# Expert biases read from SBUF at a register's address, in place of two transfers per tile

## What is computed

```python
def _moe(tokens, router_w, w1, b1, w2, b2):
    logits = tokens @ router_w.T
    probs = jax.nn.softmax(logits, axis=-1)
    rw, re = jax.lax.top_k(probs, TOP_K)            # TOP_K = 2, 8 experts
    ...
    for e in range(E):
        h = jax.nn.gelu(tokens @ w1[e] + b1[e], approximate=False)
        y = h @ w2[e] + b2[e]
        out = out + combine[:, e:e + 1] * y
    return out
```

## Time and profile before

| | us |
|---|---|
| median of three runs | 1556.3 (1552.33 to 1566.34) |
| span of the profiled execution | 1438.5 |
| median less span | 117.8 |
| TensorE busy in the span | 1290.5 (90%) |
| VectorE busy | 1128.0 (78%) |
| ScalarE busy | 991.0 (69%) |
| GpSimd busy | 753.0 (52%) |

### The profile page before, as it was taken

The page is one execution under the profiler, slowest core; times in us unless marked ns, Lnnn a source line. Parts: engine busy times, 40 slices in busy tenths (PEclk is TensorE's granted clock), DMA queues, the critical chain, the costliest instruction groups (busy, mean ns, idle before and its releaser), DMA issues. The chain is left out here.

```text
span 1438.5 us, 28829 instructions
## 1 busy us (share of the span) xinstructions
PE 1290.5 (90%) x8512; PEld 1130.8 (79%) x8512; DVE 1128.0 (78%) x3903; ACT 991.0 (69%) x2090; POOL 753.0 (52%) x963
## 2 busy tenths in 40 slices
PE   3899999999999999999999489999999999994544
PEld 3788888888888888888887378899999999993433
DVE  5478888888788878778786888899999999993332
ACT  1777677767677777676765567788888888871332
POOL 3115655666555575656555575566666666663000
PEclk9999999999999999999999779999999999996555
DMA  8622534353542222222111189988888888865999
GB/s 279 212 81 79 146 89 135 101 150 85 139 130 68 79 79 67 80 72 77 56 53 43 49 263 318 289 277 269 271 279 264 272 279 269 268 220 225 425 424 378
DMA packets 144136, 264.00 MB, mean 184 GB/s; under 512 B 52336, under 2 KB 74480, under 8 KB 139760
## 3 DMA queue, kind: packets, MB, share of 16 engines
q1 hardware_dynamic: 113440, 173.78, 38.6%
q0 software_dynamic: 25920, 71.60, 14.0%
q10 hardware_dynamic: 4624, 16.78, 2.9%
HBM read 128.39 MB, written 100.68 MB: 159 GB/s over the span
## 5 line engine op out<-in xcount | busy, mean ns | idle before, releaser
L1716 POOL DMA_INDIRECT answers<-yy,dest_i x284 | 280.3, 987 | 175.2 <-DVE yy L1837 100.8
L1558 POOL DMA_INDIRECT sent<-tn,slot_s x256 | 276.4, 1080 | 146.1 <-issue 79.3
L1768 PE MATMUL s_bank<-band,hh 128*128 x568 | 163.2, 287 | 0.6 <-DVE yy L1872 0.6
L1768 PE MATMUL s_bank<-w_s,hh 128*128 x568 | 157.2, 277 | 0.0
L1768 PE MATMUL s_bank<-band,hl 128*128 x568 | 157.0, 276 | 0.0
L1802 ACT ACTIVATE hid<-m_bank,b1s 128x512 f32<-128x512 f32 x142 | 97.9, 689 | 80.7 <-PE m_bank L1751 48.3
L1822 ACT ACTIVATE zz<-xin 128x256 f32<-128x256 f32 x284 | 147.5, 601 | 0.0
L758 PE MATMUL m_bank<-wvo,band 128*128 128x258 f32 x792 | 132.7, 303 | 13.2 <-DVE band L1390 10.9
L1535 POOL TENSOR_TENSOR rs<-ve,halves 128x4 f32<-128x4 f32 x64 | 65.0, 1020 | 150.8 <-DVE ve L1252 150.8
L790 PE MATMUL o_bank<-vv,at 128*128 128x256 f32 x512 | 140.8, 398 | 1.4 <-DVE tt L1300 0.7
L758 PEld LDWEIGHTS m_bank<-wvo,band 128*128 128x128 f32 x792 | 107.0, 191 | 29.5 <-issue 27.8
(11 more groups left out here) (238 smaller groups left out, 3655.9 us busy)
## 6 DMA issues: line engine op xcount, KB each, us to landing
xin<-sent SPq DMA_DIRECT2D x71, 524.0 KB
got<-answers SPq DMA_DIRECT2D x32, 1024.0 KB, 13.8
w1hs<-rT SPq DMA_DIRECT2D x71, 256.0 KB
w1ls<-w_s SPq DMA_DIRECT2D x71, 256.0 KB
xs<-in_x SPq DMA_DIRECT2D x32, 512.0 KB, 4.8
raw<-in_x SPq DMA_DIRECT2D x32, 512.0 KB
out_x<-fin ACTq DMA_DIRECT2D x15, 1024.0 KB, 12.4
b2s<-in_b SPq DMA_DIRECT2D x71, 128.0 KB
```

Source lines behind the costliest of these rows:

```text
L1558: eng.indirect_dma_start(sent, bass.IndirectOffsetOnAxis(slot_s[:, par, j, k:k + 1], 0), tn[:, par, k, :], None).then_inc(scattered[par], 16)
L1716: eng.indirect_dma_start(answers, bass.IndirectOffsetOnAxis(dest_i[:, at_ % RING, k:k + 1], 0), yy[:, slot, k, :], None).then_inc(rows_out ...
L1768: last = eng.matmul(y_bank[half][:, k * C:(k + 1) * C], hx[:, par, f, ts], rhs, start=(n == 0), stop=(n == 3 * CC - 1))
```

## The change

`b1_all`, the table of all experts' b1, has been in SBUF since the token loop. ScalarE now takes its bias from there: it loads the tile's expert into a register of its own and reads at that address. `b2_all` is a new buffer of 8 KB per partition in place of `b2s` (4 KB); SyncE fills it once, behind tile 0's weights, with one transfer of 1 MB that copies the whole of b2 to all partitions. VectorE also loads the expert's number itself and reads `b2_all` at that address. SyncE's transfers of `b1s` and `b2s` are gone; `w_here` counts 32 per tile in place of 64. The waits of ScalarE and VectorE on `w_here` are gone; VectorE waits for `b2_in` once.

```diff
-        b1s = eb("b1s", [P, WS, CC])
-        b2s = eb("b2s", [P, WS, C])
+        b2_all = eb("b2_all", [P, E, C])
+        b2_in = sem("b2_in")
...
-                    eng.dma_start(b1s[:, slot, :], b1_all[:, bass.ds(e, 1), :].rearrange("p e a -> p (e a)"))\
-                       .then_inc(w_here[slot], 16)
-                    eng.dma_start(b2s[:, slot, :], b2[bass.ds(e, 1), :].rearrange("e c -> (e c)").partition_broadcast(P))\
-                       .then_inc(w_here[slot], 16)
+                    if at_ == 0:
+                        eng.dma_start(b2_all[:, :, :].rearrange(flat), b2.rearrange("e c -> (e c)").partition_broadcast(P))\
+                           .then_inc(b2_in, 16)
...
-                    eng.wait_ge(w_here[at_ % WS], at_ // WS * 64 + 64)
+                    eng.wait_ge(w_here[at_ % WS], at_ // WS * 32 + 32)
...
-                    eng.wait_ge(w_here[at_ % WS], at_ // WS * 64 + 64)
+                    if at_ == 0:
+                        eng.wait_ge(w_late, 16)
+                    if at_ == WHOLE:
+                        eng.wait_ge(listed, 1)
+                    e = entry(eng, expert_i, at_, E - 1)
...
-                        eng.activation(hid[:, f, :], h_bank[f][:, :], ACT.Gelu, bias=b1s[:, at_ % WS, f:f + 1])\
+                        eng.activation(hid[:, f, :], h_bank[f][:, :], ACT.Gelu, bias=b1_all[:, bass.ds(e, 1), f:f + 1].rearrange("p e a -> p (e a)"))\
...
+                if it.runs("Y"):
+                    e = entry(eng, expert_i, it.block("Y"), E - 1)
...
-                    eng.wait_ge(w_here[at_ % WS], at_ // WS * 64 + 64)
+                    if at_ == 0:
+                        eng.wait_ge(b2_in, 16)
...
-                                          b2s[:, at_ % WS:at_ % WS + 1, :].broadcast_to([P, 2, C]),
+                                          b2_all[:, bass.ds(e, 1), :].broadcast_to([P, 2, C]),
```

## The result

The changed kernel takes 1541.6 us, median of 14 runs (1529.2 to 1550.5), beside 1556.1 us for the kernel before, 14 runs (1549.9 to 1566.3). The ratio on record is 0.9897, interval 0.987 to 0.9923: 16 us less (the two medians alone lie 14.5 us apart), where 8.5 were forecast, and 1540.3 us if the ratio is put on the shown median, just under the range of 1541 to 1564. A ratio leaves out executions that took over 1.5% more than the fastest of the same kernel on the same chip; for the changed kernel with 0.9984 these are three of ten.

The account below looks back on a forecast made before the run. TensorE bounds the expert stage's middle, SyncE's queue its early tiles, transfers the output stage. 7.15 (early tiles) + 2.05 (first gap) - 0.3 (later hid) = 8.9, less 0.4 for xin gaps: 1556.3 - 8.5 = 1547.8 us, range 1541 to 1564.

Parts of the forecast that it names:

- The early tiles: Expert stage, 851 to 909 us: SyncE's queue lags TensorE; without the two transfers all 7.15 us come back.
- The first gap: TensorE's wait before tile 1 of the expert stage: 2.05 of 2.71 us saved, about 0.7 stay.
- The 1 MB transfer and the register loads at 0: Transfer behind tile 0's weights and loads on ScalarE and VectorE are hidden by other waiting or work: cost 0.
- The price of 0.87 us for an exposed load: Upper bound for one register load on VectorE, read from SyncE's time between xin's end and w1hs.
- The exposed load: Rival, chance 0.15: VectorE's load isn't hidden, 6.75 us per tile, +24 over 60 tiles, +18 in all, 1574 us.
- The transfer-bound one: Rival, chance 0.14: early tiles stay bound by transfers, only volume counts, 1 to 4 us won, about 1553 us.
- "Nothing changes": Rival, chance 0.09: xin takes b2s's place as the last transfer to land for TensorE; 1556 us.
- 117.8 above the span: Difference between median time 1556.3 and profile span 1438.5 us: launch and surroundings, untouched by the edit.
- the middle unchanged with TensorE full: Expert stage after 909 us: TensorE busy for all 381 us, 6.35 us per tile, the same after the edit.
- The sum: Whole kernel: 7.15 + 2.05 - 0.3 = 8.9 us, less 0.4 for smaller gaps on xin: 8.5 us saved.

Follow-up runs that it names:

- the changed kernel with 0.9984: The changed kernel, unaltered, measured again on chip D as reference beside runs with added transfers or loads: ratio 0.9984 (0.9937 to 1.0030) to the kernel before.
- the second profile of before: The kernel before, no edit, profiled and timed once more on chip A: ratio 1.0016, span 1562.3 us.
- each half alone: Kernel before with only ScalarE's half (b1s transfer gone): 0.9947; with only VectorE's half (b2s transfer gone, 1 MB transfer added): 0.9982.
- the first measurement: The changed kernel against the kernel before, chip not on record: 1541.6 us beside 1556.1 us, ratio 0.9897.
- loads_only: Kernel before plus the changed kernel's register loads on ScalarE and VectorE, unused, without the 1 MB transfer: 1.0162 on chip B from four executions; repeated on chip C 1.0008.
- The measurement on chip E: The changed kernel, unaltered, measured a third time, as reference for a run without its register loads: ratio 0.9950 (0.9919 to 0.9982) to the kernel before.

## Why the prediction was off

*The early tiles: right in cause, and about right in size.* Waits on b2s of 7.9 us in the second profile of before, 2.2 us on w1ls after: 5.7 us of recorded idle time are gone. I had 9.2 by starts (7.15 + 2.05). All gaps but the first vanished, as stated, and each half alone makes most of them vanish. That the queue falls behind is shown by its rows and by those two runs.

*The first gap: mis-sized.* I expected 0.7 us of it to stay; 2.2 us stay (3.5 us before, by the second profile). The saving is 1.3 us across these two profiles, not 2.05. Whether the 1 MB transfer has a part in it was not tried.

*The 1 MB transfer and the register loads at 0: the hiding was right.* VectorE's mix starts 0.10 us behind yy as before; nothing in the middle waits for VectorE's or ScalarE's bias. The price of 0.87 us for an exposed load was too high: with its range check the load takes 0.45 us on SyncE in the trace that I had (0.273 + 0.155 + 0.018) and 0.52 us on VectorE after. With 0.47 us of room an exposed load would by that have cost 0.05 x 60 = 3 us, an estimate, not 24. What the loads may cost in another way is said under what stays open.

*The rivals.* The exposed load did not happen. The transfer-bound one did not either: with the transfers gone no early tile waits for weights. "Nothing changes" is out by the ratio in two of three measurements; the third, 0.9984, has 1 inside its interval.

*The step that failed: "117.8 above the span (launch and what else lies around it), which no part of the edit touches", and with it "the middle unchanged with TensorE full".* Around the span lie 1.7 us. The rest of the 117.8 us were pauses inside the stages, with the slow clock behind the longest, in the token loop and in the middle, where TensorE is busy for 403 of 437.7 us and not full. The sum put their reaction to the edit at nothing. Comparing the two profiles that look like the timed runs, the middle went from 437.7 to 425.0 us; of these 12.7 us I had none. That pauses react to what is issued is shown by the runs that add transfers or loads that nobody waits for. That the 16 us of the first measurement are 6 us of waits and some 8 to 10 us less in pauses is what remains by subtraction, not shown by itself. One pair of profiles can't give this to the microsecond: where both run the same code, up to tile 1's transposes, they differ by 6.6 us (882.8 and 876.2), and the first eleven tiles took 5.3 us longer after, where pauses fell, so that the two profiles differ by only 7.4 us in the whole expert stage. But in eight kernels of the first measurement and of chips A and B the middle orders itself nearly as the ratios do: 425 and 427 us for 0.9897 and 0.9892, 432 and 434 for 0.9947 and 0.9982, 438 for before, 441 and 443 for 1.0022 and 1.0013, 450 for 1.0059. The ninth, loads_only with 439 us for 1.0162, does not fit.

*Luck.* The measurement on chip E, 0.9950, is the forecast's 0.9945 within its interval. That is no support for the sum, which left out the pauses and also the price of the loads; on chip D the same sum missed to the other side.

*What stays open.* Two transfers per tile cost 0.7 to 1.3% when they are added to the changed kernel, and its loads cost 0 to 0.7%. If taking two away saves what adding two costs, that makes a gain of 0 to 1.3%, with the waits some 0.4% more. The measurements gave 0.16, 0.50 and 1.03%. On chip D the additions cost 0.7 to 1.3%, while the removal, the change itself, gained only 0.16% (between a gain of 0.6 and a loss of 0.3); why it didn't gain more there isn't explained. Nor is what a pause is. The transfers that load instructions are not it as far as the profile goes: the two queues for instructions have 73 and 79 packets in the shown profile of before, without pauses, and the same in the second one, with them. The Trainium skill (NOTIFIC — the notification-queue block, The write path) says that the block which writes the records of instructions and transfers can hold back its producers when its own pipeline is full. That would fit a cost per issued instruction on any sequencer, and would make part of the pauses an effect of recording; no run here switched the recording off, so none shows it. The shown profile of before speaks against recording as the whole cause: it was recorded too, and its middle has no pause.

## What to carry to other kernels

Before a profile is used for a sum, set its span beside the times: 118 us between them were, but for 1.7, not launch but time that this one execution lacked, in just the places where I called the engine full. A transfer that is small in bytes still costs its place in a queue: 2.2 us of issue per tile put the queue behind TensorE as soon as other work joined it. And in a kernel with such pauses, transfers and register loads that nobody waits for can still cost time (two more transfers or four more loads per tile, 0.2 to 0.35 us), so "hidden" is not yet "free". To judge them, measure the reference beside them on the same chip and look at the granted clock too.

## What the hardware showed unexpectedly

- Pauses on TensorE and ScalarE at once: ScalarE's gelu is preceded by more than 1.5 us of idle time 26 times in the 59 middle tiles, before and after alike, up to 5.5 and 5.8 us, and TensorE's restarts inside a pause lie mostly 0.7 or 1.4 us apart. The middle before takes 63 us more than in the shown profile, after 50 us.
- Behind the longest of them TensorE's granted clock falls to half for 3.4 us or more, and matmuls of 512 columns start 0.43 in place of 0.23 us apart.
- Two transfers of one 8-byte packet cost at least as much as two of 128 packets (1.0116 and 1.0085 beside 0.9984).
- A register load takes 0.305 us on VectorE and 0.325 us on ScalarE (medians), with 0.19 + 0.02 us of range check on VectorE, and the engine works on through it.
- The same kernel before takes 1556 us on two chips and 1602 to 1606 us on three others, with the same instructions.
